# Four residual convolutions on one core: the statistics of three convolutions in other slots, and x1's rows loaded ahead of x2's rows

## What is computed

```python
x = x + conv3x3_zero_pad(gn(x), L0_weights) + bias            # A
W = gn(x); X = W.T / (norm1(W) * norminf(W))                  # B, for each of the 128 matrices
for _ in range(5): X = X @ (2*I - W @ X)                      #    Newton-Schulz inverse
x = x + X
x = x + conv3x3_circular(gn(x), L2_weight)                    # C (written with FFTs)
x = x + mask(conv3x3_zero_pad(gn(x), L3_K))                   # D (last row and column masked)

def gn(v, G=8, eps=1e-5):       # mean and variance over 2 channels x 128 x 128, per image and group
    g = v.reshape(B, G, C // G, H, W)
    return ((g - mean(g)) / sqrt(var(g) + eps)).reshape(v.shape)
```

## Time and profile before

| | us |
|---|---|
| median of 3 runs | 736.62 |
| the runs | 734.77, 736.62, 741.38 |
| the profiled execution, its own time | 734.72 |
| its span in the trace | 732.6 |
| TensorE busy | 608.0 |
| DVE busy | 534.3 |
| ACT busy | 383.9 |
| GpSimd busy | 198.3 |
| DMA moved | 76.43 MB, mean 104 GB/s |

### The profile page before, as it was taken

One profiled execution on the slowest core, in us unless ns is written; L12 is line 12 of the kernel. 1 busy time (PEld: TensorE's weight loads), 2 busy tenths in 40 slices (PEclk: granted clock), 3 DMA queues, 4 the chain that ended last, 5 costly groups with the idle time before them and its releaser, 6 DMA issues.

```text
span 732.6 us, 11297 instructions
## 1 busy us (share of the span) xinstructions
PE 608.0 (83%) x3752; PEld 508.3 (69%) x3752; DVE 534.3 (73%) x1304; ACT 383.9 (52%) x559; POOL 198.3 (27%) x289
## 2 busy tenths in 40 slices
PE   0695679749999989889898989989999969995956
PEld 0464667648777778778776878778777858884644
DVE  3755976656897888797887779886978587648551
ACT  0351347424666556765756456655667436753632
POOL 5132123002252224322331315222333122201302
PEclk9997899969999999999999999999999998999888
DMA  5196001950378332960497234951363135223352
GB/s 152 52 106 183 1 30 34 132 195 30 90 89 259 87 80 57 179 180 29 111 126 215 70 83 70 201 153 43 87 211 81 44 80 166 48 76 73 85 131 57
DMA packets 89124, 76.43 MB, mean 104 GB/s; under 512 B 6572, under 2 KB 81228, under 8 KB 86252
## 3 DMA queue, kind: packets, MB, share of 16 engines
q1 hardware_dynamic: 87548, 74.07, 43.9%
q0 software_dynamic: 1536, 1.86, 1.0%
HBM read 38.14 MB, written 24.25 MB: 85 GB/s over the span
## 4 chain that ended last, share of the span: by engine, by line
PE 38%; DVE 26%; SPq 10%; DMA 8%; issue 8%; ACT 6%; POOL 3%; DVEq 0%; POOLq 0%; ACTq 0%
PE conv_ps L750 21%; DVE zl L1005 5%; DMA x<-x_dram 4%; PE z L831 3%; DMA rows_dram<-x 3%; DVE stB L676 3%; PE z L833 3%; PE z L835 3%; PE z L826 2%; PE z L840 2%; SPq L275 2%; DVE bn_D L538 2%; ACT d_A L650 2%; SPq L377 2%; POOL d_A L623 2%
## 5 line engine op out<-in xcount | busy, mean ns | idle before, releaser
L1005 DVE SCALAR_TENSOR_TENSOR zl<-z,zh 128x1024 fp32r<-128x1024 f32 x128 | 154.5, 1219 | 64.7 <-ACT zh L938 62.3
L831 PE MATMUL z<-zh 128*128 128x256 f32 x512 | 156.5, 306 | 14.9 <-DVE zl L1005 14.9
L938 ACT ACTIVATE zh<-z 128x1024 fp32r<-128x1024 f32 x128 | 130.3, 1019 | 66.9 <-PE z L835 35.5
L833 PE MATMUL z<-zl,zh 128*128 128x256 f32 x512 | 149.1, 291 | 0.0
L835 PE MATMUL z<-zh,zl 128*128 128x256 f32 x512 | 148.7, 290 | 0.0
L831 PEld LDWEIGHTS z<-zh 128*128 128x128 f32 x512 | 102.4, 200 | 23.8 <-DVE zl L1005 20.7
L750 PE MATMUL conv_ps<-d_A,w_D 128*96 128x512 f32 (+1 forms) x432 | 104.2, 390 | 17.5 <-DVE w_D L608 17.1
L750 PE MATMUL conv_ps<-d_C,w_C 128*96 128x512 f32 (+1 forms) x486 | 113.9, 381 | 0.6 <-issue 0.6
L750 PE MATMUL conv_ps<-d_A,w_A 128*96 128x512 f32 (+1 forms) x378 | 93.9, 397 | 14.8 <-DVE w_A L608 10.8
L833 PEld LDWEIGHTS z<-zl,zh 128*128 128x128 f32 x512 | 102.6, 200 | 1.0
L835 PEld LDWEIGHTS z<-zh,zl 128*128 128x128 f32 x512 | 102.4, 200 | 0.0
(11 more groups left out here) (182 smaller groups left out, 890.6 us busy)
## 6 DMA issues: line engine op xcount, KB each, us to landing
x<-x_dram SPq DMA_DIRECT2D x14, 1024.0 KB, 9.1
win_C<-rows_dram SPq DMA_DIRECT2D x40, 256.0 KB, 4.0
rows_dram<-x SPq DMA_DIRECT2D x32, 256.0 KB
win_A<-x SPq DMA_DIRECT2D x48, 160.0 KB
win_D<-out_C SPq DMA_DIRECT2D x7, 1056.0 KB, 6.8
y<-out_D SPq DMA_DIRECT2D x42, 168.0 KB, 3.8
x_dram<-out_A SPq DMA_DIRECT2D x30, 192.0 KB, 2.1
win_D<-out_C SPq DMA_DIRECT2D x14, 160.0 KB, 5.9
```

The costliest lines, as they stand in the source:

```text
L831: pe.matmul(z[s][:, m, :], zh[s][:, m, 0:128], zh[s][:, m, :], start=False, stop=True, skip_group_check=True)
L833: pe.matmul(z[s][:, m, :], zh[s][:, m, 0:128], zl[s][:, m, :], start=False, stop=True, skip_group_check=True)
L938: act.activation(zh[s][:, :, :], z[s][:, :, :], ACT.Copy, scale=ROOT[j]).then_inc(s_zh[s], 1)
L1005: dve.scalar_tensor_tensor(zl[s][:, :, :], z[s][:, :, :], ROOT[j], zh[s][:, :, :].bitcast(f32), ALU.mult, ALU.subtract).then_inc(s_zl[s], 1)
```

## The change

In the program of each engine work is dealt to other slots. On SP, `load_x1` and `load_x2` change places (but for image 0). The two small products of the norms move from `misc_ps` to `spare_ps`; the chain of the norms gets a semaphore of its own (`chain_of_norms`), since `dve_rows_B_end` now comes behind them. In slot 11 TensorE waits, ahead of A's mean, for the variance of the rows.

| work | slot before | slot after |
|---|---|---|
| TensorE: transposes of chunks 0, 1, 2, 3 | 10, 11, 14, 16 | 10, 12, 15, 17 |
| TensorE: A's mean, variance | 12, 15 | 11, 14 |
| TensorE: D's mean, variance | 22, 23 | 20, 22 |
| ACT: square root A, B, D | 15, 17, 23 | 14, 12, 22 (D's ahead of the high part) |
| DVE: absolute sums of chunks 0, 1, 2, 3 | 10, 11, 14, 17 | 10, 13, 15 (behind w_A), 17 |
| DVE: B's variance, B's end | 14, 17 | 9, 21 |
| DVE: A's statistics 2, 3, 4 and weights | 13, 14, 15 | 11, 14, 15 |
| DVE: D's statistics 1 (three parts) | 18, 19, 20 | 15, 17, 18 |
| DVE: first half of the statistics of x2's rows | 20 | 19 |
| DVE: D's statistics 2, 3, 4 and weights | 21, 22, 23 | 20, 21, 22 |

```diff
@@ sp_cycle
-            if has_C:
-                for g in range(NG):
-                    load_x2(sp, i - 1, g)
             if is_int(i, 0):
                 keep_x1(sp, i)
             if nxt:
                 load_x1(sp, i + 1)
+            if has_C:
+                for g in range(NG):
+                    load_x2(sp, i - 1, g)
@@ pe_cycle
-                if nxt and q == 11:
+                if has_A and q == 11:
+                    pe.wait_ge(sB_ve, at(1, i + 1, 1))
+                    win_mean(pe, cA, i + 2)
+                if nxt and q == 12:
                     pe_norm_T(pe, i + 1, 1)
-                if has_A and q == 12:
-                    win_mean(pe, cA, i + 2)
-                if nxt and q == 14:
+                if has_A and q == 14:
+                    win_var(pe, cA, i + 2)
+                if nxt and q == 15:
                     pe_norm_T(pe, i + 1, 2)
-                if has_A and q == 15:
-                    win_var(pe, cA, i + 2)
-                if nxt and q == 16:
+                if nxt and q == 17:
                     pe_norm_T(pe, i + 1, 3)
...
+                if has_C and q == 20:
+                    win_mean(pe, cD, i - 1)
                 if has_C and q == 22:
-                    win_mean(pe, cD, i - 1)
-                if has_C and q == 23:
                     win_var(pe, cD, i - 1)
@@ act_cycle
                 if has_C and q == 22:
+                    win_sqrt(act, cD, i - 1)
                     high_parts(act, cD, i - 1, 0)
                 if has_C and q == 23:
-                    win_sqrt(act, cD, i - 1)
                     high_parts(act, cD, i - 1, 1)
@@ dve_cycle
...
                 if has_A and q == 15:
                     win_stats_4(dve, cA, i + 2)
                     win_weights(dve, cA, i + 2)
+                if nxt and q == 15:
+                    dve_abs(dve, i + 1, 2)
+                if has_C and q == 15:
+                    win_stats_1(dve, cD, i - 1, 0)
...
                 if has_C and q == 22:
-                    win_stats_3(dve, cD, i - 1)
-                if has_C and q == 23:
                     win_stats_4(dve, cD, i - 1)
                     win_weights(dve, cD, i - 1)
```

More of the change, by code:

```diff
@@ L216, in build @@
         s_chainB = sem("chain_B")
+        s_chainN = sem("chain_of_norms")
         s_chainC = sem("chain_rows_C")
@@ L857, in pe_norm_sums @@
             pe.wait_ge(s_Ta, at(NCHK, b, NCHK))
-            pe.transpose(misc_ps[0:2 * C, M_NT:M_NT + 128], sums[:, :, :].rearrange("p a c -> p (a c)"), ident)\
+            pe.transpose(spare_ps[0:2 * C, 0, :], sums[:, :, :].rearrange("p a c -> p (a c)"), ident)\
                 .then_inc(s_nT, 1)
@@ L863, in pe_norm_spread @@
             pe.wait_ge(s_dg, at(1, b, 1))
-            pe.matmul(misc_ps[:, M_NB:M_NB + 2 * C], ones_all[0:2 * C, :], diag[:, :],
+            pe.matmul(spare_ps[:, 1, 0:2 * C], ones_all[0:2 * C, :], diag[:, :],
                       start=True, stop=True).then_inc(s_nB, 1)
@@ L963, in act_cycle @@
                     high_parts(act, cA, i + 2, {14: 0, 15: 1, 17: 2, 18: 3, 19: 4, 20: 5}[q])
-                if has_A and q == 15:
+                if has_A and q == 14:
                     win_sqrt(act, cA, i + 2)
-                if nxt and q == 17:
+                if nxt and q == 12:
                     act_sqrt(act, sB_ve, sB_sd, tB[:, 3, :], tB[:, 2, :], i + 1)
                 if has_C and q == 22:
+                    win_sqrt(act, cD, i - 1)
                     high_parts(act, cD, i - 1, 0)
                 if has_C and q == 23:
-                    win_sqrt(act, cD, i - 1)
                     high_parts(act, cD, i - 1, 1)
@@ L996, in build @@
         NROW_B = NROW + 1
-        perB = NROW_B + 3
+        perN = 3
         perRC = NROW + 7
@@ L1031, in dve_norm_top @@
         def dve_norm_top(dve, b):
-            link = Chain(dve, s_chainB, perB, b, NROW_B)
+            link = Chain(dve, s_chainN, perN, b)
             dve.wait_ge(s_nT, at(1, b, 1))
-            link(dve.tensor_reduce(top[:, :], misc_ps[0:2 * C, M_NT:M_NT + 128], AX.X, ALU.max))
+            link(dve.tensor_reduce(top[:, :], spare_ps[0:2 * C, 0, :], AX.X, ALU.max))
             dve.tensor_scalar(diag[:, :], ident[0:2 * C, 0:2 * C], top[:, :], None, ALU.mult)\
@@ L1039, in dve_norm_scale @@
         def dve_norm_scale(dve, b):
-            link = Chain(dve, s_chainB, perB, b, NROW_B + 1)
+            link = Chain(dve, s_chainN, perN, b, 1)
             dve.wait_ge(s_nB, at(1, b, 1))
-            link(dve.tensor_copy(norms[:, :], misc_ps[:, M_NB:M_NB + C]))
-            link(dve.scalar_tensor_tensor(scl[:, 0, :], norms[:, :], -1.0, misc_ps[:, M_NB + C:M_NB + 2 * C],
+            link(dve.tensor_copy(norms[:, :], spare_ps[:, 1, 0:C]))
+            link(dve.scalar_tensor_tensor(scl[:, 0, :], norms[:, :], -1.0, spare_ps[:, 1, C:2 * C],
                                           ALU.mult, ALU.mult))
@@ L1141, in dve_cycle @@
                     win_stats_1(dve, cA, i + 2, 2)
+                if nxt and q == 9:
+                    dve_rows_B_var(dve, link_B, i + 1)
                 if has_C and q == 9:
@@ L1147, in dve_cycle @@
                     low_parts(dve, cC, i - 1, 4)
-                if nxt and q == 11:
-                    dve_abs(dve, i + 1, 1)
-                if has_A and q == 13:
+                if has_A and q == 11:
                     win_stats_2(dve, cA, i + 2)
@@ L1153, in dve_cycle @@
                     low_parts(dve, cC, i - 1, 5)
-                if nxt and q == 14:
-                    dve_abs(dve, i + 1, 2)
+                if nxt and q == 13:
+                    dve_abs(dve, i + 1, 1)
                 if has_A and q == 14:
                     win_stats_3(dve, cA, i + 2)
-                if nxt and q == 14:
-                    dve_rows_B_var(dve, link_B, i + 1)
                 if has_A and q == 15:
@@ L1162, in dve_cycle @@
                     win_weights(dve, cA, i + 2)
+                if nxt and q == 15:
+                    dve_abs(dve, i + 1, 2)
+                if has_C and q == 15:
+                    win_stats_1(dve, cD, i - 1, 0)
                 if nxt and q == 17:
                     dve_abs(dve, i + 1, 3)
-                    dve_rows_B_end(dve, link_B, i + 1)
+                if has_C and q == 17:
+                    win_stats_1(dve, cD, i - 1, 1)
+                if has_C and q == 18:
+                    win_stats_1(dve, cD, i - 1, 2)
                 if nxt and q == 18:
                     dve_norm_top(dve, i + 1)
-                if has_C and q == 18:
-                    win_stats_1(dve, cD, i - 1, 0)
                 if nxt and q == 19:
                     dve_norm_scale(dve, i + 1)
-                if has_C and q == 19:
-                    win_stats_1(dve, cD, i - 1, 1)
-                if has_C and q == 20:
-                    win_stats_1(dve, cD, i - 1, 2)
-                if q == 20:
+                if q == 19:
                     dve.wait_ge(s_x2, at(NCHK, i, 2))
                     row_stats_1(dve, x2, stC, sC_bn, 0)
+                if has_C and q == 20:
+                    win_stats_2(dve, cD, i - 1)
+                if nxt and q == 21:
+                    dve_rows_B_end(dve, link_B, i + 1)
                 if has_C and q == 21:
-                    win_stats_2(dve, cD, i - 1)
+                    win_stats_3(dve, cD, i - 1)
                 if has_C and q == 22:
-                    win_stats_3(dve, cD, i - 1)
-                if has_C and q == 23:
                     win_stats_4(dve, cD, i - 1)
```

6 lines of the change are left out of this document (3 added, 3 removed).

## The result

The changed kernel takes 752.16 us (750.97 to 752.96) where the kernel before takes 735.69 (728.57 to 741.38) in the same comparison: ratio 1.0264, 95% interval 1.022 to 1.0309. It is slower by 2.6%. The forecast was 745.0. Its profiled execution has a span of 750.1 us against 732.6, 17.5 more, and the mean granted clock is 0.942 against 0.952.

A forecast was written before the change was run, and what follows sets the result against it. TensorE, busy 608.0 of 732.6 us, sets the pace. From 734.7: +1.0 (cycle 0), +6.2 (cycles 1 to 5), +7 (clock), -4.0 (ends) make +10.2, 744.9, stated as 745.0; range 733 to 753.

The forecast's parts named there:

- The standstill in slot 17: TensorE's last transpose waits 4.7 us for sums behind w_A, cycles 0 to 5; loss 1.6 us in that slot.
- The clock: Half clock behind slot 17's waits, 1.6 us a time; five more such waits, about 7 us net.
- w_D: D's weights, slots 22 to 1: no gain, convolution D then waits about 1.5 us for x2; +1.2 per cycle taken.
- the upper end: The higher of two estimates of a cycle's lengthening, +0.5 and +1.4 us.
- the collision with GpSimd: D's Newton steps and weights, 3.24 us before; w_D might come a microsecond sooner where GpSimd runs nothing beside it.
- The wait for x2 in slot 1: Update of x2's chunk 3 stands behind w_D on DVE; TensorE waits about 1.5 us before convolution D.
- The swap: x1's load ahead of x2's windows on SP: x1 sooner, windows 2.9 us later; gain 0.45 us per cycle.
- both loops: TensorE's loop longer by 1.2 us a cycle, the SP load loop by 1.7 - 0.45; about 1.25 taken.
- Cycle 6: This cycle has no convolution A; forecast -0.2 us.
- Cycle 7: D's statistics fit idle DVE time in slots 16 to 19; 3.8 us of waits at and before w_D go.
- The rival "same": Slot 17 wait comes, clock falls no oftener than now, w_D quick: 735 to 739 us; chance 0.38.
- The rival "faster": x1 does not delay the windows, slot 8's waits nearly go: 723 us, 730 with clock loss; chance 0.13.

The follow-up runs named there:

- e5: Changed kernel plus 18 unread products on TensorE ahead of slot 17's last transpose; 739.87 us, ratio 1.0125 to the kernel before.
- e6: Changed kernel with GpSimd's product DS cut to one column per block after image 0; 744.54 us, ratio 1.0173 to the kernel before.
- e7: Changed kernel with D's last statistics step and weights on DVE in slot 23 instead of 22; 748.91 us, ratio 1.0246 to the kernel before.
- e1: Kernel before with only SP's swap, x1's load ahead of x2's windows; 728.67 us, ratio 0.9945 to the kernel before.
- e9: e8 with B's end on DVE moved from slot 20 to slot 17; 720.06 us, ratio 0.9809 to the kernel before.
- e3: Changed kernel with D's statistics, square root and weights in their old slots, B's end in slot 20; 754.95 us, ratio 1.0328 to the kernel before.
- e4: Kernel before with only the norms' transposes and their absolute sums moved to the new slots; 766.81 us, ratio 1.0507 to the kernel before.
- e8: Changed kernel with chunk 2's sums in slot 14, D's work in its old slots and B's end in 20; 721.66 us, ratio 0.9877 to the kernel before.
- e2: Changed kernel with chunk 2's absolute sums back in DVE's slot 14; 729.69 us, ratio 0.9983 to the kernel before.

## Why the prediction was right or wrong

The direction and, in slot 17, the mechanism were right; the size was half of what came: +8.4 us over the median shown (736.62), against +16.5 in the comparison. By its steps:

- **The standstill in slot 17: right.** Forecast 4.7 us in place of 2.07 and 0.55, measured 4.3 to 5.4 in six cycles, 27.9 in all (forecast 27). With the clock's part taken away (e5) the stretch is +9.0 us, as forecast.
- **The clock: right in its price, a little short in its sum.** Forecast 1.6 us a time and about 7 net. In cycle 3 the stretch from slot 8 to convolution A is +3.4, and +1.9 with the clock up (e5), which leaves 1.5; over six cycles it is 9.3, 1.6 a time, and 12 with all that e5 gains over the run. The saying of the Trainium skill, page "TensorE: Matmul & The Clock Gate", section "HAM oscillation — how this bites in real kernels", that a wait between bursts brings every burst in cold, would charge all six waits, and here it holds for all six: 0.50 behind each. Waits of 2.07 us do not always bring it.
- **w_D, the step that failed.** "I take +1.2, a little inside the upper end, which holds the collision with GpSimd that the row of before contains." The collision was seen in one place, the Newton steps and weights. But the move also carries D's eight middle operations, which I didn't cost, into the time of DS. In slot 20 instead of 21 they last 5.6 us instead of 1.9. D's variance is then late: TensorE waits 1.2 us in slot 22 of each cycle, and the sum had -0.4 a cycle for the stretch from convolution A to D. It came out as +3.9 us over five cycles where -2 was forecast; without DS it is -2.0 (e6). This term is 5.9 us. The wait for x2 in slot 1, forecast at 1.5, is 1.66 and right; e7 shows it to be a trade against w_D.
- **The swap: wrong in size, on the good side.** I let x1's 2.9 us stand in full before the windows, and had both loops lengthen by 1.25 us a cycle. The first half holds where the swap stands alone: the windows land 2.7 us later (e1). In the kernel after, the last window load of cycle 3 is issued at 320.8 and lands 4.1 later, 15.8 us behind convolution D's start at 309.13, only 1.0 later than before. The second half failed. TensorE's waits for D's variance and for x2 put convolution D off, and x1's load, the first of the queue's, is issued 5.8 us behind its start, where the first load of the queue came 7.2 behind it in the kernel before and 7.5 in e1. I expected ACT to wait for win_C in most cycles; it does so two times, 10.2 us in all and 9.1 of it in cycle 1. The stretch up to slot 8 is 6.0 us shorter. In cycle 3 TensorE waits there 0.87 instead of 1.52, in cycle 4 0.86 instead of 3.05, and I had no term for the clock of 0.50 that stood behind the waits of cycles 4 and 5 and goes with them (e1). The loop is not far off, though: in e9, which is 6 us faster ahead of it, it binds in part.
- **Cycle 6: wrong.** Forecast -0.2, measured +3.3. I asked only for convolution A there, but the transposes for the norms and the trade of w_D against x2 are in this cycle too. Three rows of TensorE in the kernel after, of slot 17 of cycle 6 and slots 0 and 1 of cycle 7:

```profile
605.02 0.63 PE L853 MATMUL spare_ps<-cst,DN 128*128 128x128 f32 x4 [1.15 <-DVE sums L1032]
...
624.77 0.63 PE L824 MATMUL z<-cst,DS 128*128 128x128 f32 x4 [1.09 <-DVE x L1022]
...
629.52 1.09 PE L824 MATMUL z<-cst,DS 128*128 128x128 f32 x4 [3.23 <-DVE x L1022]
```

The late sums are worth 1.0 (e3 and e4, which have them and not D's move, are at +1.0), and w_D ahead of x2's last chunk most of the rest: behind it the cycle is at +0.9 (e7). DS has a part in this, since without it the cycle is at +2.3 (e6). Cycle 7 brought 2.8 of the 3.8 forecast, and only with D's move in it.

So the sum missed 5.9 (D beside DS), 3.5 (cycle 6), 2.3 up to convolution A and 1.0 (cycle 7), and had 6.0 too little from the swap. With the 0.6 of start and end this is the difference of 17.5 and 10.2. The rival "same" named the clock as the point of decision, and e5 shows that it would have come nearly true with a clock that stays up: 1.0125. The rival "faster" asked for windows by 315, 16.4 us behind convolution D's start. They land at 15.8, but not by its mechanism: x1 does hold them back (e1), and it is convolution D that starts later. What came of it was 5 to 6 us and not 14.

Luck has a part in the number: the swap's 6.0 us, which the sum did not have, hid nearly half of what it missed elsewhere.

## What to carry to other kernels

When an operation is moved behind another, ask which buffer it releases: here two reductions of 0.68 us, one slot later in DVE's queue, held a transpose, the transpose held all of TensorE for 4.5 us, and the clock doubled the bill. A move is judged only beside the others: D's earlier statistics made no difference that could be told while TensorE stood still (e3) and cost 8 us once it did not (e8 against e2). And where small operations move, look at what GpSimd runs in their new place, since their durations in the old trace hold only for the old place.

## What the runs showed of the hardware

- **Small DVE operations end with GpSimd's.** Two-input operations on one or two columns take 0.16 to 0.22 us alone and 0.95 beside a GpSimd product of 1.02 us per instruction; in cycle 3 of the kernel after each of four operations ends within 0.1 us of one of GpSimd's. With those products shrunk the 0.95 becomes 0.16 (e6). The Trainium skill, page "SBUF — State Buffer", section "Who interferes with whom", says that the port pair shared by the two engines is an exclusive lock, taken by a DVE instruction with two SBUF inputs against a GpSimd instruction that reads SBUF. The trace agrees. It shows the same for a TENSOR_SCALAR on two columns whose scalar is a column (L561, 1.08 us beside DS; L557, 0.61 beside d_A; 0.22 each in e8, where GpSimd is idle).
- **Work that nothing reads can pay.** 18 products of 128x128, 4.18 us in each of six standstills, made the kernel 12.3 us faster (10 by the ratios); the granted clock behind them stayed at 1.00, where it was 0.50 behind each standstill. It is no remedy here: taking the standstill away (e2) gives 22.
